# Deformable convolution on one core: the offsets' rows are requested from ScalarE instead of SP

## The chip, the cores and the metric

One core of one Trainium2 chip runs the whole kernel. The metric is the device time of one execution in microseconds (us); lower is better. Engines are named as in the profile: PE (TensorE), ACT (ScalarE), DVE (VectorE), POOL (GpSimd), SP (SyncE, which here only requests DMAs).

## The reference

The input `x` is 8 images of 32 channels by 128 x 128, float32. Two residual layers follow one another:

```
x = x + L0_conv(group_norm(x))     # a spectral layer: 16 modes along each axis, plus a 1x1 mix
x = x + L1_conv(group_norm(x))     # a modulated deformable 3x3 convolution
```

With 32 groups of one channel, the group norm is a norm over each channel plane. The second layer first makes, with a plain 3x3 convolution `w_om`, 27 numbers for each pixel: two offsets and one mask value for each of the 9 taps. It then samples the image bilinearly at the offset place of each tap, multiplies by sigmoid(mask), and sums over taps and channels with `weight`. This second layer takes nearly all of the time, and the change is in it.

## The kernel before, in words

The images are cut into 2 groups of 4 images, and 4 images x 32 channels fill 128 partitions. A first stage (up to about 280 us) loads both groups, makes the first layer's output `x1`, stores it to DRAM (`x1_d`), and stores the normalised rows with a zero border to DRAM as `xh_d` (tensor `xh_scratch` in the profile).

The second layer then walks over sets. A set is 2 image rows of a group (`TILE_R = 2`). There are `NSET = 65` sets for a group (64 pairs of rows and one that only finishes), so 130 in all. Each engine has its own function `step(N, ...)` which is called for N = -3 to 130. The helper `steps` writes the first and last few steps out ("peeled") and puts the rest into a loop. The engines are tied together by semaphores only; each engine does its own instructions in the order in which they are written. In PE's step N (L1085 to L1110) the work for several sets is woven together:

- `gather` (L1026, 64 matmuls, 4 times a step) applies the sampling weights to the transposed tiles, and `spread` (L1005, 64 matmuls, 3 times) makes those weights' layout; `turn_rows` (L1035, 4 times) transposes image tiles.
- `convolve(N - 1)` (L1080, 144 matmuls) is the last product of set N - 1.
- `offsets(N + 3)` (L1047, 24 recorded matmuls) comes right behind it: the 3x3 convolution for the offsets of the set three ahead, into the PSUM tile `pM`. It reads the SBUF buffer `wino`, which holds, for 3 row shifts, the rows of that set. `wino` is a part of the large tile `big`, so the profile calls its loads `big<-xh_scratch`. There is one such buffer.
- `turn_offsets(N + 3)` (L1057) brings the offsets into another order.

What the other engines do with it: ACT copies `pM` with a bias to `om_s` (L623), and in the same step copies results of `gather` (L588, `samples`), of `spread` (L593 and L594, `table`) and of `turn_rows` (L599, `turned`). DVE copies the other halves (L758, L763), transposes products (L769), and in `output(N - 1)` writes `outs` (L780) and `begun` (L785) from what `convolve(N - 1)` left. POOL cuts the image window into tiles (L502) and makes products (L490).

What sets the order around the change is SP's step. It requests everything that the second layer loads and stores, in one fixed order: the window of set N + 1 (L390), the rows of `x1` for set N (L418, two DMAs), the output rows of set N - 1 (L425, two DMAs, behind a wait for `outs`, L422), and last the rows for the offsets of set N + 3 (L402, three DMAs, behind a wait for `om_done`). That last part is

```python
wait(sp, om_done, n)
sp.nop(nofuse=True)
for ky in range(KS):
    rows = xh_d[g * P:(g + 1) * P, bass.ds(src + (TOP - 1 + ky) * PADC, TILE_R * PADC)]
    sp.dma_start(wino[ky * C:(ky + 1) * C, :, :, :] ...).then_inc(wino_ld, 16)
```

and PE waits for it with `pe.wait_ge(wino_ld, n * (16 * KS) + 16 * KS)` at L1043. `steps` has an argument `apart`: with True the loop is broken at the border between the two image groups and the steps around it are written out; SP and DVE used it, ACT, POOL and PE did not. At the border one step has no output to store.

Of the kernel before, what the change touches and what calls it, by code (L numbers as in the profile page):

```python
# [15 lines left out]
C = 32  # L16
H = W = 128
IPG = 4
P = IPG * C
HW = H * W  # L20
MODES = 16
KS = 3
# [4 lines left out]
TILE_R, TILE_C = 2, 4  # L27
# [3 lines left out]
TOP, LEFT = 3, 4  # L31
PADR = TOP + H + TOP
PADC = LEFT + W + LEFT
# [3 lines left out]
NSET = NPAIR + 1  # L37
# [24 lines left out]
RING = 4  # L62
# [10 lines left out]
def build(nc, g_count, x, wxr, wxi, wyr, wyi, mixt, mixb, womt, bom, wct, biasc,  # L73
          dft, inv, ident_d, perm, sel, cols, gtab, out):
    ctx = ExitStack()
    with ctx:
# [6 lines left out]
        def sem(name):  # L83
            return ctx.enter_context(nc.semaphore(name))
# [3 lines left out]
        xh_d = nc.dram_tensor("xh_scratch", (g_count * P, PADR * PADC), fp32, kind="Internal").ap()  # L88
# [18 lines left out]
        wino = areas[6].rearrange("p (b r x) -> p b r x", b=IPG, r=TILE_R)  # L107
# [112 lines left out]
        xh_st = [sem(f"xh_st{i}") for i in range(2)]  # L220
        pad_st = sem("pad_st")

        win_ld = [sem(f"win_ld{i}") for i in range(2)]
        wino_ld = sem("wino_ld")
        x1_ld = [sem(f"x1_ld{i}") for i in range(2)]
        out_st = [sem(f"out_st{i}") for i in range(2)]
        om_done = sem("om_done")
# [41 lines left out]
        N_XH = H // XHR  # L269
        SETS = g_count * NSET  # L270
# [3 lines left out]
        def wait(eng, s, v):  # L274

            if not (isinstance(v, int) and v <= 0):
                eng.wait_ge(s, v)
# [54 lines left out]
        def _(sp):  # L332
# [20 lines left out]
            for b in range(IPG):  # L353
                r, m = slice(b * C, (b + 1) * C), slice(b * C, b * C + OMC)
# [6 lines left out]
            for ky in range(KS):  # L361
                r, k = slice(ky * C, (ky + 1) * C), slice(ky * KS, (ky + 1) * KS)
# [28 lines left out]
                             xh_d[g * P:(g + 1) * P, bass.ds(local * (TILE_R * PADC), WIN_R * PADC)]) \  # L391
                    .then_inc(win_ld[q], 16)

            def load_rows(n, place):

                g, local = place(n)
                src = local * (TILE_R * PADC)
                wait(sp, om_done, n)
                sp.nop(nofuse=True)
                for ky in range(KS):  # L400
                    rows = xh_d[g * P:(g + 1) * P, bass.ds(src + (TOP - 1 + ky) * PADC, TILE_R * PADC)]
                    sp.dma_start(wino[ky * C:(ky + 1) * C, :, :, :].rearrange("c b r x -> c b (r x)"),  # L402
                                 rows.rearrange("(b c) n -> c b n", b=IPG)).then_inc(wino_ld, 16)

            def halves_of(t, g, pair, i):

                return t[g * P:(g + 1) * P, bass.ds(pair * PX + i * W, W)].rearrange("(r p) n -> p r n", r=2)

            def step(N, s, on, place):
                q = s % 2  # L410
                if on[1]:
                    load_window(N + 1, 1 - q, place)
                g, local = place(N)
                if on[0] and not (isinstance(local, int) and local == NPAIR):
                    wait(sp, conv_read, N - 1)
                    sp.nop(nofuse=True)
                    for i in range(TILE_R):
                        sp.dma_start(x1r[i * HALF:(i + 1) * HALF, q, :, :], halves_of(x1_d, g, local, i)) \  # L418
                            .then_inc(x1_ld[q], 16)
                g, local = place(N - 1)  # L420
                if on[-1] and not (isinstance(local, int) and local == 0):
                    sp.wait_ge(out_ready, N - 1 - g)  # L422
                    sp.nop(nofuse=True)
                    for i in range(TILE_R):
                        sp.dma_start(halves_of(out, g, local - 1, i), outs[i * HALF:(i + 1) * HALF, 1 - q, :, :]) \  # L425
                            .then_inc(out_st[1 - q], 16)
                if on[3]:
                    load_rows(N + 3, place)
            steps(sp, step, 2, True)
            for q in range(2):  # L430
                sp.wait_ge(out_st[q], 16 * NPAIR * g_count)
# [118 lines left out]
        @block.scalar  # L550
        def _(act):
            act.wait_ge(const_ld, 16 * NCONST)
            def deviation(g, n):
                act.wait_ge(aggr, n * g_count + g + 1)
                nc.scalar.activation(col1[:, g, 5 * n:5 * n + 1], mv[:, g, 1:2], ACT.Sqrt,
                                     bias=cols_s[:, 3:4]).then_inc(sd_done, 1)

            for g in range(g_count):
                deviation(g, 0)
            act.wait_ge(zeroed, 1)  # L560

            def normalize(g, j, q):

                nc.scalar.activation(
                    stg[:, q, :, LEFT:LEFT + W],
                    X[g][:, bass.ds(j * (2 * XHR * W) + q * XHR * W, XHR * W)]
                    .rearrange("p (a b) -> p a b", b=W),
                    ACT.Identity, bias=col1[:, g, 7:8], scale=col1[:, g, 6:7]).then_inc(xh_done, 1)

            for g in range(g_count):  # L570
                deviation(g, 1)
                act.wait_ge(norm1, g + 1)
                first = 0
                if g == 0:
                    for q in range(2):
                        normalize(g, 0, q)
                    first = 1
                with act.Fori(first, N_XH // 2) as j:
                    for q in range(2):
                        act.wait_ge(xh_st[q], (j + g * (N_XH // 2)) * 16)  # L580
                        normalize(g, j, q)
            act.wait_ge(x1_st, 16 * LOADS * g_count)
            act.wait_ge(blocks_ld, 16 * NBLOCK)

            def samples(n, k):

                act.wait_ge(v_done, n * TCH + (k + 1))
                nc.scalar.activation(*evacuate(k, 0), ACT.Copy).then_inc(v_act, 1)  # L588

            def table(n, j):  # L590

                act.wait_ge(e_done, n * ROUNDS + (j + 1))
                nc.scalar.activation(*unit_of(j, 0, 0), ACT.Copy)  # L593
                nc.scalar.activation(*unit_of(j, 1, 0), ACT.Copy).then_inc(e_act, 1)  # L594

            def turned(n, k):

                act.wait_ge(t_done, n * TCH + (k + 1))
                nc.scalar.activation(XT[:, k * 512:(k + 1) * 512], pR[:, :], ACT.Copy).then_inc(xt_done, 1)  # L599

            def step(N, s, on, place):
                if on[-1]:
                    samples(N - 1, 2)
                if on[0]:
                    table(N, 0)
                    turned(N, 2)
                if on[-1]:
                    samples(N - 1, 3)
                if on[2]:
                    act.wait_ge(sub_done, N + 3)  # L610
                    nc.scalar.activation(U, U, ACT.Abs).then_inc(abs_done, 1)
                if on[0]:
                    turned(N, 3)
                    table(N, 1)
                if on[2]:
                    act.wait_ge(abs_done, N + 3)
                    wait(act, prod_done, N * KS)
                    nc.scalar.activation(HT[:, :, (s + 2) % RING, :],
                                         U.rearrange("p (f n) -> p f n", f=2 * KS), ACT.Relu,
                                         bias=cols_s[:, 1:2], scale=-1.0).then_inc(lin_done, 1)  # L620
                if on[3]:
                    act.wait_ge(om_done, N + 4)
                    nc.scalar.activation(  # L623
                        om_s[:, :].rearrange("p (i j t) -> p i j t", i=TILE_R, t=NT),
                        pM[:, 0:PX].rearrange("p (i t j) -> p i j t", i=TILE_R, t=NT),
                        ACT.Identity, bias=bom_s[:, 0:1]).then_inc(om_act, 1)
                if on[0]:
                    samples(N, 0)
                    table(N, 2)
                if on[1]:  # L630
                    turned(N + 1, 0)
                if on[0]:
                    samples(N, 1)
                if on[1]:
                    turned(N + 1, 1)
                if on[3]:
                    act.wait_ge(omT_done, N + 4)
                    wait(act, hats_done, N + 2)
                    nc.scalar.activation(msk[:, 1 - s % 2, :], pM[:, 2 * KS * PB:3 * KS * PB],  # L639
                                         ACT.Sigmoid).then_inc(msk_done, 1)  # L640
            steps(act, step, RING)

            act.wait_ge(flag_set, 1)
            far = act.value_load(flag_i[0:1, 0:1], min_val=0, max_val=1)
            with act.If(far > 0):
                for i in range(images):
                    m = g_sem[i // IPG]
                    at0 = (i % IPG) * H
                    with act.Fori(0, H) as y:
                        act.wait_ge(m["own"], y * OWN + (at0 * OWN + 1))  # L650
                        nc.scalar.activation(g_mask, g_om[:, 2 * TAPS:OMC], ACT.Sigmoid).then_inc(m["act"], 1)
# [556 lines left out]
```

## Time and profile before

| | us |
|---|---|
| median of 2 runs (3114.12 to 3114.29) | 3114.2 |
| the profiled execution's own time | 3112.75 |
| its span, first to last instruction | 3110.7 |
| PE busy | 2128.6 (68%) |
| DVE busy | 1373.5 (44%) |
| ACT busy | 1159.8 (37%) |
| POOL busy | 890.1 (29%) |
| mean granted TensorE clock | 0.818 of full |

Busy time of an engine is the sum over its own instructions; the requests of DMAs are not counted in it. The mean granted clock is a share of 2.4 GHz. The second layer fills the span from about 280 us to the end.

### The profile page before, as it was taken

What the parts mean: (1) busy time and instruction counts of PE and PEld (TensorE: products, weight loads), DVE (VectorE), ACT (ScalarE), POOL (GpSimd) and SP (SyncE); (2) the same over time, 40 slices, a digit from 0 to 9 for tenths busy, and PEclk for the clock granted to TensorE, in tenths of its full rate; (3) what the DMA queues carried; (4) which work ended last, traced back from release to release, by engine and by line L of the source; (5) the groups of instructions that cost most, each with busy time, mean ns of one, the idle gap of its engine ahead of it and who ended that gap; (6) DMA issues with size and microseconds to landing.
All of it is one profiled execution on the core that took longest, in us unless ns stands there. A gap on an engine that the chain in (4) does not pass through costs nothing.

```text
span 3110.7 us, 187708 instructions
## 1 busy us (share of the span) xinstructions
PE 2128.6 (68%) x83517; PEld 1562.6 (50%) x83517; DVE 1373.5 (44%) x2326; ACT 1159.8 (37%) x2378; POOL 890.1 (29%) x1153
## 2 busy tenths in 40 slices
PE   7653666766767667676676767676676766767666
PEld 3312544555545555455555555455554555545454
DVE  9692333434434344344444444343443444434443
ACT  0024333433434344343443444343443434434343
POOL 0001223323233232332323332332323323233231
PEclk9795788888888887888878888888878888788888
DMA  6165112121121211212112111212112121121210
GB/s 238 58 249 187 37 45 57 42 56 50 49 56 42 56 49 49 56 42 56 49 50 55 55 50 49 56 42 56 49 49 56 42 56 49 50 56 42 56 50 25
DMA packets 161699, 196.30 MB, mean 63 GB/s; under 512 B 20288, under 2 KB 136672, under 8 KB 157536
## 3 DMA queue, kind: packets, MB, share of 16 engines
q1 hardware_dynamic: 161632, 195.34, 21.2%
q8 instruction: 50, 0.82, 0.1%
q14 instruction: 17, 0.14, 0.0%
HBM read 143.05 MB, written 52.22 MB: 63 GB/s over the span
## 4 chain that ended last, share of the span: by engine, by line
PE 55%; DMA 12%; issue 10%; SPq 10%; ACT 7%; DVE 6%; DVEq 1%; ACTq 0%
PE pE L1005 14%; PE pM L1047 12%; DMA big<-xh_scratch 11%; PE pVV L1026 10%; PE pVV L1080 9%; PE pR L1035 7%; SPq L425 6%; SPq L402 4%; ACT big L599 3%; ACT big L594 3%; PE pM L1057 2%; DVE outs L780 2%; DVE big L736 2%; DMA xh_scratch<-win 1%; DVEq L736 1%
## 5 line engine op out<-in xcount | busy, mean ns | idle before, releaser
L1047 PE MATMUL pM<-big,wom 96*32 96x256 f32 x3120 | 358.6, 628 | 826.0 <-DMA big<-xh_scratch 826.0
L502 POOL COPY big<-win 128x480 f32<-128x480 f32 x520 | 289.5, 587 | 1830.3 <-PE pR L1035 1817.6
L758 DVE COPY big<-pVV 128x288 f32<-128x288 f32 x520 | 232.7, 447 | 1223.2 <-PE pVV L1026 1222.9
L1047 PEld LDWEIGHTS pM<-big,wom 96*32 96x32 f32 x3120 | 128.7, 164 | 977.5 <-DMA big<-xh_scratch 791.6
L1026 PE MATMUL pVV<-big 60*32 60x72 f32 x33280 | 511.0, 253 | 16.7 <-issue 14.6
L623 ACT ACTIVATE om_s<-pM,bom_s 128x256 f32<-128x256 f32 x130 | 61.8, 476 | 1215.2 <-PE pM L1047 1215.2
L490 POOL TENSOR_TENSOR prod<-big 128x600 f32<-128x600 f32 (+1 forms) x489 | 504.1, 1040 | 0.0
L1026 PEld LDWEIGHTS pVV<-big 60*32 60x32 f32 x33280 | 407.9, 116 | 177.9 <-issue 172.2
L763 DVE COPY big<-pE 128x768 f32<-128x768 f32 x390 | 368.7, 945 | 229.7 <-PE pE L1005 229.7
L1005 PE MATMUL pE<-big,sel_s 32*64 32x96 f32 x24960 | 449.5, 274 | 20.4 <-issue 10.3
L1005 PEld LDWEIGHTS pE<-big,sel_s 32*64 32x64 f32 x24960 | 372.8, 145 | 86.7 <-issue 71.2
L769 DVE STREAM_TRANSPOSE big<-prod 128x768 f32<-128x768 f32 x390 | 377.6, 968 | 0.2 <-DVE outs L780 0.2
L1035 PE MATMUL pR<-ident,big 128*128 128x128 f32 x2080 | 362.8, 300 | 17.8 <-ACT big L599 1.6
L599 ACT ACTIVATE big<-pR 128x512 f32<-128x512 f32 x520 | 310.3, 597 | 43.2 <-PE pR L1035 38.3
L1080 PE MATMUL pVV<-big,wc 64*32 64x128 f32 x18720 | 297.5, 272 | 11.3 <-issue 10.5
L588 ACT ACTIVATE big<-pVV 128x288 f32<-128x288 f32 x520 | 214.0, 412 | 208.3 <-PE pVV L1026 204.5
L593 ACT ACTIVATE big<-pE 128x384 f32<-128x384 f32 x390 | 199.4, 511 | 232.9 <-PE pE L1005 232.9
L1035 PEld LDWEIGHTS pR<-ident,big 128*128 128x128 f32 x2080 | 232.1, 148 | 96.1 <-ACT big L599 54.5
L1080 PEld LDWEIGHTS pVV<-big,wc 64*32 64x32 f32 x18720 | 260.0, 106 | 29.5 <-issue 14.4
L594 ACT ACTIVATE big<-pE 128x384 f32<-128x384 f32 x390 | 195.4, 501 | 0.0
L780 DVE SCALAR_TENSOR_TENSOR outs<-pVV,bias_s,begun 128x256 f32<-128x256 f32 x128 | 61.9, 483 | 180.3 <-PE pVV L1080 180.3
L801 DVE TENSOR_TENSOR big<-pM,cols_s 128x720 f32<-128x720 f32 x130 | 116.7, 898 | 55.2 <-ACT msk L639 55.2
(75 smaller groups left out, 1147.7 us busy)
## 6 DMA issues: line engine op xcount, KB each, us to landing
big<-xh_scratch SPq DMA_DIRECT2D x390, 136.0 KB, 2.6
win<-xh_scratch SPq DMA_DIRECT2D x130, 408.0 KB, 3.5
xh_scratch<-win SPq DMA_DIRECT2D x32, 544.0 KB, 2.7
big<-in_x SPq DMA_DIRECT2D x16, 1024.0 KB, 15.7
x_scratch<-big SPq DMA_DIRECT2D x16, 1024.0 KB, 3.9
x1r<-x_scratch SPq DMA_DIRECT2D x256, 64.0 KB, 3.0
out<-outs SPq DMA_DIRECT2D x256, 64.0 KB, 2.1
xh_scratch<-zero SPq DMA_DIRECT2D x4, 204.0 KB, 2.7
```

What stands on the lines that cost most here:

```text
L490: made = nc.gpsimd.tensor_tensor(prod[:, kx, at:at + m, 0:SQ].rearrange("p m (a b) -> p m a b", a=NSH), hy.to_broadcast(shape), hx.to_broa ...
L502: last = nc.gpsimd.tensor_copy(strips[:, half * HTP:(half + 1) * HTP, h, 0:REG].rearrange("p t (r x) -> p t r x", r=WIN_R), tiles_of(q, h, ...
L594: nc.scalar.activation(*unit_of(j, 1, 0), ACT.Copy).then_inc(e_act, 1)
L599: nc.scalar.activation(XT[:, k * 512:(k + 1) * 512], pR[:, :], ACT.Copy).then_inc(xt_done, 1)
L758: nc.vector.tensor_copy(*evacuate(k, 1)).then_inc(v_dve, 1)
L763: nc.vector.tensor_copy(*both_units(j, 2)).then_inc(e_dve, 1)
L769: nc.vector.transpose(PT[:, kx, :], prod[:, kx, :, :].rearrange("p m k -> p (m k)")) \
L1005: last = mm(o[:, i2::TILE_R], sel_s[part, i2 * KS + kx, :], src[:, i2::TILE_R, :, t0:t0 + HTP], start=True, stop=True)
L1026: last = mm(o[:, :, t * TILE_C:(t + 1) * TILE_C, :], XT[part, x:x + C], A[part, at, :], start=True, stop=True)
L1035: last = nc.tensor.transpose(pR[:, u * P:(u + 1) * P], strips[:, k * TPC + u, :, :].rearrange("p h x -> p (h x)"), ident[:, :])
L1047: last = mm(pM[b * C:(b + 1) * C, 0:PX], wom[:, kx, :], wino[0:KS * C, b, :, x0:x0 + W], start=(kx == 0), stop=(kx == KS - 1))
L1080: last = mm(pV[r][to:to + C, c:c + W], wc[part, PLACES[at][1] * KS + kx, o * C:(o + 1) * C], VS[part, m, kx, :], start=(at == same[0] and ...
```

## The change

`load_rows` leaves SP's step and goes to ACT, right behind the copy of the offsets (L623). It is called for the next set, N + 4, so it is requested when `offsets(N + 3)` has finished reading the buffer, and no longer behind SP's output stores. The rows of set 0 are requested before ACT's first step. ACT's steps are now also written out at the border of the groups (`apart` is True), since the address depends on the group. PE, DVE and POOL are unchanged.

```diff
@@ SP
-            def load_rows(n, place):
-
-                g, local = place(n)
-                src = local * (TILE_R * PADC)
-                wait(sp, om_done, n)
-                sp.nop(nofuse=True)
-                for ky in range(KS):
-                    rows = xh_d[g * P:(g + 1) * P, bass.ds(src + (TOP - 1 + ky) * PADC, TILE_R * PADC)]
-                    sp.dma_start(wino[ky * C:(ky + 1) * C, :, :, :].rearrange("c b r x -> c b (r x)"),
-                                 rows.rearrange("(b c) n -> c b n", b=IPG)).then_inc(wino_ld, 16)
-
...
-                if on[3]:
-                    load_rows(N + 3, place)
             steps(sp, step, 2, True)
@@ ACT
+            def load_rows(n, place):
+
+                g, local = place(n)
+                src = local * (TILE_R * PADC)
+                for ky in range(KS):
+                    rows = xh_d[g * P:(g + 1) * P, bass.ds(src + (TOP - 1 + ky) * PADC, TILE_R * PADC)]
+                    nc.scalar.dma_start(wino[ky * C:(ky + 1) * C, :, :, :].rearrange("c b r x -> c b (r x)"),
+                                 rows.rearrange("(b c) n -> c b n", b=IPG)).then_inc(wino_ld, 16)
+
...
+            act.wait_ge(pad_st, 16 * 2 * g_count)
+            for q in range(2):
+                act.wait_ge(xh_st[q], 16 * (N_XH // 2) * g_count)
+            load_rows(0, lambda n: divmod(n, NSET))
 
             def step(N, s, on, place):
...
                         ACT.Identity, bias=bom_s[:, 0:1]).then_inc(om_act, 1)
+                    if not isinstance(N, int) or N + 4 < SETS:
+                        load_rows(N + 4, place)
                 if on[0]:
                     samples(N, 0)
...
-            steps(act, step, RING)
+            steps(act, step, RING, True)
```

## Rows read from the trace of the kernel before

**Rows 1.** The page: the chain that ended last, its shares by engine

```profile
PE 55%; DMA 12%; issue 10%; SPq 10%; ACT 7%; DVE 6%; DVEq 1%; ACTq 0%
```

**Rows 2.** The waits, 404.5 to 3034.05 us (us in total, times, longest)

```profile
PE pM L1047 <- DMA big<-xh_scratch: 765.2, 122, 6.6
```

**Rows 3.** The chain, 1634 to 1644 us (start us, us, what)

```profile
1634.91 2.21 PE pVV L1080 x144
...
1637.15 0.49 DVE outs L780
...
1637.71 0.63 SPq L425
...
1638.39 0.63 SPq L425
...
1639.11 0.55 SPq L402
...
1639.70 0.44 SPq L402
...
1640.19 2.81 DMA big<-xh_scratch
1643.00 0.04 issue
1643.04 2.79 PE pM L1047 x24
```

**Rows 4.** Windows: length; PE, PEld, DVE, ACT, POOL busy; granted clock, DMA share, GB/s

```profile
1617.00:1618.00 1.00, 0.00 (x0) 0.00 (x0) 0.08 (x1) 0.00 (x0) 0.00 (x0) 0.79 0.27 66
1741.37:1754.58 13.21, 12.99 (x643) 10.48 (x638) 8.84 (x13) 8.56 (x18) 7.04 (x11) 1.00 0.03 10
1621.33:1643.04 21.71, 15.61 (x638) 11.83 (x639) 9.04 (x14) 8.67 (x18) 6.68 (x8) 0.81 0.20 54
```

**Rows 5.** The timeline of the step at the border of the groups (start us, us)

```profile
1739.20 2.25 PE L1080 MATMUL pVV<-big,wc 64*32 64x128 f32 x144
...
1741.37 1.50 PE L1047 MATMUL pM<-big,wom 96*32 96x256 f32 x24
1741.50 0.43 DVE L785 TENSOR_TENSOR begun<-pVV,x1r 128x256 f32<-128x256 f32 x1 [1.24 <-PE pVV L1080]
1742.94 0.48 ACT L623 ACTIVATE om_s<-pM,bom_s 128x256 f32<-128x256 f32 x1 [1.97 <-PE pM L1047]
1743.81 0.41 ACT L588 ACTIVATE big<-pVV 128x288 f32<-128x288 f32 x1 [0.39 <-PE pVV L1026]
1744.70 0.51 ACT L593 ACTIVATE big<-pE 128x384 f32<-128x384 f32 x1 [0.48 <-PE pE L1005]
1745.11 0.51 ACT L594 ACTIVATE big<-pE 128x384 f32<-128x384 f32 x1
1745.48 0.61 ACT L599 ACTIVATE big<-pR 128x512 f32<-128x512 f32 x1
1746.14 0.66 PE L1035 MATMUL pR<-ident,big 128*128 128x128 f32 x4
1746.93 1.11 POOL L502 COPY big<-win 128x480 f32<-128x480 f32 x2 [3.75 <-PE pR L1035]
1752.36 2.25 PE L1080 MATMUL pVV<-big,wc 64*32 64x128 f32 x144
```

**Rows 6.** The timeline of SP, the same stretch and behind it

```profile
1729.59 1.28 SPq L402 DMA_DIRECT2D big<-xh_scratch  x3
1755.21 1.29 SPq L425 DMA_DIRECT2D out<-outs  x2
1756.60 1.52 SPq L402 DMA_DIRECT2D big<-xh_scratch  x3
1758.22 0.38 SPq L390 DMA_DIRECT2D win<-xh_scratch  x1
1758.69 1.31 SPq L418 DMA_DIRECT2D x1r<-x_scratch  x2
```

**Rows 7.** The page: DMA issues, KB each, median us from issue to landing

```profile
big<-xh_scratch SPq DMA_DIRECT2D x390, 136.0 KB, 2.6
win<-xh_scratch SPq DMA_DIRECT2D x130, 408.0 KB, 3.5
```

**Rows 8.** The timeline of PE: the ninth and the last of the 130 offsets' convolutions

```profile
432.49 2.79 PE L1047 MATMUL pM<-big,wom 96*32 96x256 f32 x24 [6.31 <-DMA big<-xh_scratch]
...
3034.05 2.79 PE L1047 MATMUL pM<-big,wom 96*32 96x256 f32 x24 [6.02 <-DMA big<-xh_scratch]
```

**Rows 9.** The timeline of PE, two waits for code in written-out steps

```profile
312.72 0.34 PE L1026 MATMUL pVV<-big 60*32 60x72 f32 x10 [1.64 <-issue]
...
3050.03 1.72 PE L1080 MATMUL pVV<-big,wc 64*32 64x128 f32 x100 [1.56 <-issue]
```

**Rows 10.** A window behind the first of them, columns as in rows 4

```profile
314.00:315.00 1.00, 1.00 (x36) 0.93 (x36) 0.00 (x0) 0.50 (x2) 1.00 (x3) 0.50 0.12 25
```

## Prediction

> **What bounds the kernel now.** I read the chain that ended last first. PE holds 55% of it, but DMA 12%, SP 10% and issue 10% also stand in it [rows 1], and a kernel bound by PE alone would have none of these. The waits say where they come from: in the loop PE sat idle 765.2 us in 122 waits for the rows of the offsets' convolution, so 6.27 us in each step [rows 2]. The chain of one step shows why [rows 3]. `convolve` ends at 1637.12. DVE writes `outs` (0.49 us), SP issues two output stores (1.3 us) and only then the three loads of rows, and the last one lands 2.81 us after its issue. At 1643.04 PE goes on, 5.9 us after it stopped. Nothing in the rows loaded depends on those outputs. SP's fixed order alone put them behind.
>
> The stall has a second cost. While PE is idle the granted clock falls (0.79 in a window inside the stall of another step), and the mean over a stalled step is 0.81 against 1.00 in a step without the stall [rows 4]. The convolution takes 2.79 us after a stall and 1.50 us without one [rows 3, 5].
>
> The border of the image groups is a natural experiment. There one step has no output to store, so SP requested the next rows early, at 1729.59 [rows 6], and at 1741.37 the convolution follows `convolve` at once [rows 5]. From that start to the start of the next `convolve` is 10.99 us, and from a `convolve` to the convolution behind it 2.17 us (1739.20 to 1741.37), so a step without the stall is 13.16 us. The mean step is (3034.05 - 432.49) / 121 = 21.50 us [rows 8]: from the ninth to the last of 130 convolutions.
>
> **The change, part by part.** All durations are of the profiled execution: span 3110.7 us, own time 3112.75, 1.45 below the median of 3114.2. So span + 2.05 + 1.45 compares with the median.
>
> *The stall goes.* The rows will be requested behind the offsets' copy, 1.57 us after `convolve` ends (1742.94 against 1741.37 [rows 5]), for use a full step later, some 11 us after the request. A load of rows lands 2.6 us after issue, the larger window load 3.5 [rows 7]. The stall of 6.27 us is gone, and so are the 2.07 us that a stalled step loses besides (21.50 - 13.16 - 6.27, the slow clock). The loop costs 121 x 13.16 = 1592.4 instead of 2601.6 us: 1009.2 saved, if nothing is added.
>
> *Outside the loop.* The steps ahead of it have four such waits, 6.31 us the last [rows 8], 24 us together. But their code is written out and PE also waits for code there, 1.56 and 1.64 us at a time [rows 9], and the stalls gave time to fetch it. I take 17 of the 24 (bounds 5 and 30), and 1.6 us for the warm clock behind the last convolution: 18.6.
>
> *SP.* The three issues (1.52 us) leave it [rows 6]. Window and `x1` loads move up by as much behind the outputs. What is late next there? POOL's tiles need the window 5.56 us after `convolve` ends (1746.93 - 1741.37 [rows 5]). SP will issue it at 0.6 + 1.3 + 0.1 = 2.0 us after that end, and it lands at 5.5, later if ACT's 408 KB share the way. A delay of 1 us costs nothing: POOL is busy 7 of 13.2 us [rows 4]. DVE's and POOL's work that now lies in the stall is `outs`, `begun`, a transpose and a product, and at the border the same transpose and product ran beside the convolution with no wait of PE. I cost this at 0.
>
> *ACT gets three issues.* No DMA is issued by ACT before, so I bound it. SP's three take 1.28 to 1.52 us, plus 0.1 to form addresses [rows 6]. Behind L623 ACT next owes L588, which it ran at 1743.81. L588 may start as late as 1744.3 (1744.70 less its 0.41) before it delays L593, and L593, L594, L599 are a tight chain on which the transpose at 1746.14 waits [rows 5]; each delay there is a delay of PE. If the issues start as L623 does, at 1742.94, they end at 1744.32 to 1744.56: up to 0.25 us lost. If they start when L623 has ended, at 1743.42, they end at 1744.8 to 1745.04: 0.5 to 0.75 lost. The bounds are 0 and 0.75 us a step, unless issuing is slower there than on SP. I take 0.4, the middle: x 121 = 48.4 us.
>
> L594 starts 0.40 us after L593, which lasts 0.51 [rows 5], so ACT's queue is ahead of its engine. The Trainium skill (Perfetto Trace Analysis, "DVE / Act Engine Instruction") says that the sequencer pushes an instruction into a wait queue and is then free for the next; by that rule the issues run beside L623 and the loss is the lower one, which would give about 2100 us; no run before shows it with a DMA.
>
> *The sum.* 3110.7 - 1009.2 - 18.6 + 48.4 = 2131.3 span, + 2.05 + 1.45 = 2135 us, 31% less. With a loss of 0 it is 2086, with 0.75 it is 2177: the forecast's own range is 2080 to 2180. The extra steps written out at the border for ACT (nine, little code) I cost at nothing; DVE and SP had them, and no wait of PE shows it.
>
> **The rivals.** *A. Issues of SP and ACT get in each other's way.* Before, one engine issued all; now SP issues stores, window and `x1` loads from 0.6 to about 3.7 us after `convolve` (1.29 + 0.38 + 1.31 with gaps [rows 6]), and ACT begins at 1.7. If one has to wait while the other issues, ACT's three wait for what is left of a store (0.25), the window (0.38) and one `x1` load (0.65): 1.3 us more. They end at 4.4 us, and L588's limit is 2.93 (1744.3 - 1741.37). The loss is 1.35 to 1.5 a step instead of 0.4. Time: 2086 + 121 x 1.35 = 2250 us. For it: in rows 6 no two issues ever lie over one another, but one engine made them all, so the trace can't tell. Against it: nothing. 
>
> *B. The clock stays low.* A single wait for code of 1.64 us [rows 9] was followed by a window at 0.50 [rows 10], although PE was busy in most of the time around it. If the smaller gaps left in each step do the same, the 2.07 us a step stay: 2135 + 250 = 2385 us. Against it: the border's step ran at 1.00 with ACT's short waits in it [rows 4].
>
> *C. Slower: ACT is held until its loads have landed.* Three times 2.6 us [rows 7] from 1.67 us on end at 9.5, 6.5 us past the limit of 2.93. PE would be idle as long as now, at another place, and the clock fall with it: 13.16 + 6.5 + 2.07 = 21.7 us a step, against 21.50: about 3140 us. With the window's 3.5 us each it is 24.4 us a step and 3465. It decides from 6.3 us of delay on ACT. For it: only that no issue on ACT was ever seen. Against: on SP an issue (0.5 us) returns long before the landing.
>
> *D. The rows are late all the same.* Landing would have to take 11 us instead of 2.6. Nothing speaks for it; then it stays near 3114.
>
> **How the numbers follow.** Forecast 0.62, A 0.23, B 0.08, C 0.03, D 0.02; 0.02 is left for a time under 2080. The predicted time is the forecast's 2135. The range takes in the forecast and A: 2075 to 2255. Faster by over 2% (which is about what a measurement of this kernel can tell from no change) are all but C and D: 0.95. D and the mild half of C are within 2%: 0.03. Slower: 0.02.
>
> **What would show it.** In the profile after, the wait of PE L1047 for the DMA is gone in the loop, L1047 takes 1.50 us, the mean clock is above 0.97, and a step is 13.2 to 13.9 us. PE L1035 waits for ACT L599 some tenths of a us once a step; that is the loss I took as 0.4, and its size tells the two bounds apart. Under A ACT's three issues last over 2.5 us instead of 1.5, in alternation with SP's, and the step is 14.5 us. Under B the step is over 15 us with a clock near 0.85. I am wrong altogether if PE's wait for DMA comes back under another name, such as POOL's for the window leading to PE's, or if PE's time in a step without waits isn't 13.2 us.

## The result and the profile after

| | before | after |
|---|---|---|
| median, us | 3114.2 (2 runs) | 2102.1 (2101.17 to 2103.03, 2 runs) |
| span of the profiled execution | 3110.7 | 2099.3 |
| mean granted TensorE clock | 0.818 | 0.96 |

The ratio is 0.6748, with a 95% interval of 0.6732 to 0.6764: the changed kernel takes a third less time. 2135 us was predicted, in a range of 2075 to 2255. One execution below is left aside: the first profile of e3_act_late was taken in a slow state (2996.9 us at a granted clock of 0.672), where the five other executions of that kernel took 2937 to 2950 us.

First the page of the kernel after: busy times, and the chain that ended last by engine.

```profile
PE 1876.1 (89%) x83517; PEld 1449.4 (69%) x83517; DVE 1372.3 (65%) x2326; ACT 1144.4 (55%) x2378; POOL 888.6 (42%) x1153
...
PE 58%; ACT 14%; issue 11%; ACTq 6%; DVE 5%; DMA 2%; DVEq 2%; SPq 0%; POOL 0%; POOLq 0%
```

Where [rows 1] had DMA with 12% and SP with 10%, there are now 2% and 0%. PE's busy time itself fell, from 2128.6 to 1876.1 us, for the same 83517 matmuls: that is the clock. ACT has 14% instead of 7%.

The waits of the kernel after, over its loop (413.16 to 2024.96 us, from the ninth to the last convolution), those that matter:

```profile
POOL big L489 <- DMA win<-xh_scratch: 715.6, 120, 7.8
...
PEld pR L1038 <- ACT big L595: 58.5, 230, 0.3
```

PE's wait for the rows [rows 2] isn't in this list at all. PE still waits for ACT's copy L595 (L599 of the kernel before), about half a microsecond a step in its weight loads, but that is no price of the change: the loop of a kernel in which ACT issues nothing (e11, below) has 57.4 us of it. POOL now waits for the window, which it did not before; that costs the kernel nothing, as below.

Windows of the kernel after, columns as in rows 4: a step in the loop, a step near the border that is written out, and the whole loop.

```profile
1106.76:1120.18 13.42, 12.99 (x643) 10.49 (x639) 8.97 (x14) 8.45 (x18) 6.65 (x9) 1.00 0.31 82
1239.28:1252.44 13.16, 12.98 (x642) 10.52 (x638) 8.98 (x14) 8.52 (x18) 6.84 (x10) 1.00 0.30 83
413.16:2024.96 1611.80, 1574.16 (x77203) 1271.20 (x77199) 1085.69 (x1692) 1022.94 (x2178) 819.54 (x1058) 1.00 0.30 82
```

The mean step is 1611.80 / 121 = 13.32 us against 21.50, at full clock. The written-out step takes exactly the 13.16 that the border's step of [rows 5] gave. Only ACT's, SP's and DVE's code is written out there; PE's and POOL's is still the loop.

The timeline of that written-out step, to set beside [rows 3, 5]:

```profile
1239.28 1.50 PE L1050 MATMUL pM<-big,wom 96*32 96x256 f32 x24
...
1239.96 1.30 SPq L414 DMA_DIRECT2D out<-outs  x2
...
1240.85 0.47 ACT L624 ACTIVATE om_s<-pM,bom_s 128x256 f32<-128x256 f32 x1 [1.97 <-PE pM L1050]
1240.85 1.35 ACTq L578 DMA_DIRECT2D big<-xh_scratch  x3
...
1241.35 0.55 SPq L390 DMA_DIRECT2D win<-xh_scratch  x1
...
1242.25 0.41 ACT L584 ACTIVATE big<-pVV 128x288 f32<-128x288 f32 x1 [0.93 <-PE pVV L1029]
...
1242.61 0.51 ACT L589 ACTIVATE big<-pE 128x384 f32<-128x384 f32 x1
...
1243.09 0.93 PE L1029 MATMUL pVV<-big 60*32 60x72 f32 x64
...
1246.98 1.12 POOL L489 COPY big<-win 128x480 f32<-128x480 f32 x2 [5.76 <-DMA win<-xh_scratch]
```

Three things are to be seen. The convolution (1.50 us) stands right behind `convolve`. ACT's three issues begin at the same instant as the copy L624 and end at 1242.20, after its engine has long been free; L584 starts at 1242.25, 0.05 us behind them, and early enough for PE's second `gather` (L1029), which stands 3.81 us behind the start of the convolution, as in the border's step before (1745.18 against 1741.37):

```profile
1745.18 0.89 PE L1026 MATMUL pVV<-big 60*32 60x72 f32 x64
```

And ACT's first issue lies over SP's store, which ended at 1241.26: both engines are issuing at the same time.

The same place in a step of the loop:

```profile
1108.33 0.48 ACT L624 ACTIVATE om_s<-pM,bom_s 128x256 f32<-128x256 f32 x1 [1.97 <-PE pM L1050]
1108.58 1.37 ACTq L578 DMA_DIRECT2D big<-xh_scratch  x3
...
1110.05 0.41 ACT L584 ACTIVATE big<-pVV 128x288 f32<-128x288 f32 x1 [1.25 <-PE pVV L1029]
...
1110.82 0.87 PE L1029 MATMUL pVV<-big 60*32 60x72 f32 x64 [0.18 <-issue]
```

Here the issues start 0.25 us behind the copy's start instead of with it; in most steps of the loop it is 0.15 to 0.16. In the loop the address is formed from the loop's register, and the trace has register instructions of L578 there; in a written-out step the address is a constant, and it has none. L584 starts 1.72 us behind L624 instead of 1.40, and the second `gather` 4.06 us behind the convolution's start (1106.76) instead of 3.81.

This is the whole loss. In 115 of the 121 steps from the ninth copy of the offsets to the last, a step takes the time from L624 to L584 plus 11.70 us, to within 0.03: 13.27 us with 1.57, 13.35 with 1.65, 13.41 with 1.71. Where L584 comes within 1.46 us, the step is 13.15 to 13.17.

### The profile page after: what moved, and what is told of

It is laid out like the page before. It is cut to its first block, busy times and chain, and to the rows that moved or that the text cites. A ratio compares the mean times of both kernels' runs of the same rounds, so it can differ in the third digit from the quotient of the medians.

```text
span 2099.3 us, 187393 instructions
## 1 busy us (share of the span) xinstructions
PE 1876.1 (89%) x83517; PEld 1449.4 (69%) x83517; DVE 1372.3 (65%) x2326; ACT 1144.4 (55%) x2378; POOL 888.6 (42%) x1153
## 4 chain that ended last, share of the span: by engine, by line
PE 58%; ACT 14%; issue 11%; ACTq 6%; DVE 5%; DMA 2%; DVEq 2%; SPq 0%; POOL 0%; POOLq 0%
PE pE L1008 14%; PE pVV L1083 14%; PE pM L1050 9%; PE pR L1038 9%; PE pVV L1029 8%; ACTq L578 6%; ACT big L595 5%; ACT big L590 5%; PE pM L1060 4%; DVE big L739 3%; ACT big L589 3%; DMA xh_scratch<-win 1%; DVEq L739 1%; DVE stats L674 1%; DMA win<-xh_scratch 1%
## 5 line engine op out<-in xcount | busy, mean ns | idle before, releaser
L1029 PE MATMUL pVV<-big 60*32 60x72 f32 x33280 | 469.2, 231 | 33.5 <-issue 26.5
L1029 PEld LDWEIGHTS pVV<-big 60*32 60x32 f32 x33280 | 377.0, 106 | 144.9 <-issue 138.3
L1008 PE MATMUL pE<-big,sel_s 32*64 32x96 f32 x24960 | 413.3, 255 | 17.0 <-issue 7.6
L1008 PEld LDWEIGHTS pE<-big,sel_s 32*64 32x64 f32 x24960 | 341.1, 131 | 73.5 <-issue 46.7
L1038 PE MATMUL pR<-ident,big 128*128 128x128 f32 x2080 | 345.4, 289 | 20.2 <-ACT big L595 1.9
L584 ACT ACTIVATE big<-pVV 128x288 f32<-128x288 f32 x520 | 214.0, 412 | 267.0 <-PE pVV L1029 255.4
L595 ACT ACTIVATE big<-pR 128x512 f32<-128x512 f32 x520 | 311.7, 599 | 38.9 <-PE pR L1038 38.3
L1038 PEld LDWEIGHTS pR<-ident,big 128*128 128x128 f32 x2080 | 220.9, 142 | 97.0 <-ACT big L595 62.0
L1050 PE MATMUL pM<-big,wom 96*32 96x256 f32 x3120 | 199.3, 387 | 52.1 <-DMA big<-xh_scratch 50.2
L624 ACT ACTIVATE om_s<-pM,bom_s 128x256 f32<-128x256 f32 x130 | 61.8, 475 | 272.8 <-PE pM L1050 272.8
L1050 PEld LDWEIGHTS pM<-big,wom 96*32 96x32 f32 x3120 | 88.3, 109 | 125.4 <-issue 76.5
L804 DVE TENSOR_TENSOR big<-pM,cols_s 128x720 f32<-128x720 f32 x130 | 116.7, 898 | 57.4 <-ACT msk L642 57.4
```

Source lines behind the costliest of these rows:

```text
L1008: last = mm(o[:, i2::TILE_R], sel_s[part, i2 * KS + kx, :], src[:, i2::TILE_R, :, t0:t0 + HTP], start=True, stop=True)
L1029: last = mm(o[:, :, t * TILE_C:(t + 1) * TILE_C, :], XT[part, x:x + C], A[part, at, :], start=True, stop=True)
L1038: last = nc.tensor.transpose(pR[:, u * P:(u + 1) * P], strips[:, k * TPC + u, :, :].rearrange("p h x -> p (h x)"), ident[:, :])
L1050: last = mm(pM[b * C:(b + 1) * C, 0:PX], wom[:, kx, :], wino[0:KS * C, b, :, x0:x0 + W], start=(kx == 0), stop=(kx == KS - 1))
```

## The experiments

The theory after the result: the gain is that the rows are asked for before the outputs are waited for, whoever asks; PE's own 13.16 us are then the floor of a step, and the 0.16 above it is ACT's address work and issues, which use up all of ACT's slack behind the offsets' copy. The rival: the second queue, ACT's, is what helps.

**e1_sp_head** and **e2_sp_before_out**: only SP's order, on the kernel before.

```diff
             def step(N, s, on, place):
                 q = s % 2
+                if on[3]:                      # e1_sp_head
+                    load_rows(N + 3, place)
                 if on[1]:
                     load_window(N + 1, 1 - q, place)
...
                         sp.dma_start(x1r[...]) .then_inc(x1_ld[q], 16)
+                if on[3]:                      # e2_sp_before_out
+                    load_rows(N + 3, place)
                 g, local = place(N - 1)
...
-                if on[3]:
-                    load_rows(N + 3, place)
             steps(sp, step, 2, True)
```

> The kernel before, but SP requests the offsets' rows at the head of its step, one set's time earlier, instead of last; ACT issues nothing and isn't written out at the border. Theory (the gain is that the rows are requested before the outputs are waited for, whoever issues): PE's wait for the rows goes, the step is 13.16 us and not the 13.32 of the changed kernel, since ACT has no issues on it: 121 x 0.16 = 19 us under the 2102 of the changed kernel, about 2085. Rival (a second queue is needed, because SP's three issues more delay the window or the x1 rows until PE waits for them): over 2150.

> As e1_sp_head, but the rows are requested behind the window and the x1 rows, just ahead of the wait for the outputs: the smallest edit of SP's order. Theory: the same 2085, and POOL's wait for the window is shorter than in e1_sp_head, because the window is requested first. Rival (the window's landing matters): this one is faster than e1_sp_head by over 10 us.

Measured: e1 2085.3 us (ratio 0.6705, 0.6694 to 0.6716), e2 2081.2 us (0.6687, 0.6675 to 0.6698). Both are where the theory put them, and the rival is out: SP alone, with no other queue, has the whole gain. The mean step is 13.21 and 13.18 us. e2 is 4 us faster, not 10, and the two intervals overlap, though in e1 POOL waits 9.8 us at worst for its window and in e2 4.9.

**e3_act_late**, run again as **e9_act_late_again**: the change's other half alone. ACT issues, but late, for set N + 3 and behind the outputs.

```diff
-            load_rows(0, lambda n: divmod(n, NSET))
...
                 if on[3]:
+                    wait(act, om_done, N + 3)
+                    g, local = place(N - 1)
+                    if on[-1] and not (isinstance(local, int) and local == 0):
+                        act.wait_ge(out_ready, N - 1 - g)
+                    act.nop(nofuse=True)
+                    load_rows(N + 3, place)
                     act.wait_ge(om_done, N + 4)
...
-                    if not isinstance(N, int) or N + 4 < SETS:
-                        load_rows(N + 4, place)
```

> The changed kernel, but ACT requests the rows late again: those of set N + 3, behind a wait for the outputs of set N - 1. So only the issuer is changed. Theory (the issuer is worth only the 1.3 us of SP's two stores, which no longer stand ahead): PE's stall is 0.6 + 1.35 + 2.6 = 4.6 us, with the slow clock's 2.07 behind it a step is 19.8 us: about 2900. Rival (ACT's own queue is what helps): near 2100.

> The kernel of e3_act_late once more, whose two times lay 60 us apart at a granted clock of 0.672 in the profile. Theory: undisturbed, the stall is 4.6 us and the slow clock's 2.07 us comes with it as in the kernel before, 2900 to 2940, mean clock near 0.80. Rival (a stall at this place costs more than before): it stays at 2970 or above.

Measured: 2937.2 us the first time and 2942.3 (2938.4 to 2949.8) the second, ratio 0.9459 (0.9443 to 0.9475), 2 us above the range that was expected. The timeline of the second:

```profile
1237.14 2.25 PE L1086 MATMUL pVV<-big,wc 64*32 64x128 f32 x144
1239.54 0.48 DVE L786 SCALAR_TENSOR_TENSOR outs<-pVV,bias_s,begun 128x256 f32<-128x256 f32 x1 [1.33 <-PE pVV L1086]
1240.24 1.41 ACTq L578 DMA_DIRECT2D big<-xh_scratch  x3
1240.25 1.49 SPq L414 DMA_DIRECT2D out<-outs  x2
...
1242.66 1.49 SPq L407 DMA_DIRECT2D x1r<-x_scratch  x2
1243.88 2.79 PE L1053 MATMUL pM<-big,wom 96*32 96x256 f32 x24 [4.49 <-DMA big<-xh_scratch]
```

The stall is 4.49 us (4.6 expected) with the convolution at 2.79 us again. The mean step of the loop is 20.00 us (19.8 expected). So to change the issuer alone is worth 5%, 1.5 us a step, about the length of SP's stores; to ask early is worth the rest. This timeline also settles rival A: the three issues of ACT and the two of SP run fully beside one another. ACT's take 1.41 us, where SP's three took 1.28 and 1.52 alone [rows 6]. SP's two take 1.49, more than the 1.29 of rows 6, but not because of ACT: the next pair, L407, takes 1.49 as well, 1 us after ACT's last issue ended, and the median of one store issue is 0.65 us in this kernel and in the kernel before.

**e4_apart_only**: the kernel before with only ACT's steps written out at the border (`steps(act, step, RING, True)`).

> The kernel before with only ACT's steps written out at the border of the groups. Theory: no change, 3110 to 3118. Rival (fetching ACT's extra code costs or helps): off by more than 10 us.

Measured: 3111.75 us, ratio 1.0004 (0.9993 to 1.0014), as expected. It costs nothing.

**e5_six_halves**: each of ACT's loads in two, by images.

```diff
                 for ky in range(KS):
-                    rows = xh_d[g * P:(g + 1) * P, ...]
-                    nc.scalar.dma_start(wino[ky * C:(ky + 1) * C, :, :, :] ...)
+                    for h in range(2):
+                        rows = xh_d[g * P + h * 64:g * P + (h + 1) * 64, ...]
+                        nc.scalar.dma_start(wino[ky * C:(ky + 1) * C, 2 * h:2 * h + 2, :, :] ...)
...
-                pe.wait_ge(wino_ld, n * (16 * KS) + 16 * KS)
+                pe.wait_ge(wino_ld, n * (32 * KS) + 32 * KS)
```

> The changed kernel with each of ACT's three loads cut into two (six issues, the same bytes). Theory (ACT's slack behind L624 is used up by three issues, so that every further 0.1 us there is 0.1 us of PE): if an issue has a fixed cost of 0.45 us, six take 2.7, 1.35 more, and the time is 2102 + 121 x 1.35 = 2265; if half of it goes with the rows moved, 2180. Rival (ACT has slack to spare): 2102 to 2115.

Measured: 2356.8 us, 255 more than the changed kernel and 92 over the highest number expected. Its timeline:

```profile
1245.57 0.47 ACT L625 ACTIVATE om_s<-pM,bom_s 128x256 f32<-128x256 f32 x1 [1.97 <-PE pM L1051]
1245.72 3.03 ACTq L579 DMA_DIRECT2D big<-xh_scratch  x6
...
1248.79 0.41 ACT L585 ACTIVATE big<-pVV 128x288 f32<-128x288 f32 x1 [2.75 <-issue]
...
1249.56 0.88 PE L1030 MATMUL pVV<-big 60*32 60x72 f32 x64 [1.68 <-ACT big L585]
```

Six issues of half the rows take 3.03 us in this step, and 2.83 us in many others of the loop; three of whole rows take 1.36 to 1.37 in most steps of the changed kernel's loop. That is 0.47 to 0.50 us an issue against 0.46, so the price is for the issue and hardly for the rows. PE waits 1.68 us for ACT's copy, in the second `gather`. The rule of the changed kernel holds here too: 14.72 us a step with L585 3.02 us behind the copy. On the mean L585 starts 3.18 us behind it instead of 1.62, which makes 188 of the 257 us that the loop is longer: the theory's 1.35 a step, a little larger. The rest, 68 us, is the clock. Two windows of the same kernel, one with the end of that gap (1249.56) in it and one 2.4 us behind that end:

```profile
1249.00:1250.00 1.00, 0.44 (x43) 0.47 (x46) 0.18 (x1) 1.00 (x4) 0.00 (x0) 1.00 0.99 327
1252.00:1253.00 1.00, 1.00 (x43) 0.93 (x48) 0.00 (x0) 0.23 (x1) 1.00 (x3) 0.50 0.00 0
```

In 54 of the 121 steps the clock falls to half behind the gap and in 67 it does not. The first take 16.22 us on the mean, the others 14.82, and together 15.44. The expectation had left that out.

**e6_copy_beside** and **e7_copy_behind**: one more copy on ACT, which nobody reads, before or behind the three issues.

```diff
+                    nc.scalar.activation(spare[:, :, :], wc[:, 0:4, :] ..., ACT.Copy)    # e6
                     if not isinstance(N, int) or N + 4 < SETS:
                         load_rows(N + 4, place)
+                    nc.scalar.activation(spare[:, :, :], wc[:, 0:4, :] ..., ACT.Copy)    # e7
```

> The changed kernel with one more ACT copy of 128x256 (some 0.45 us), which nobody reads, between the offsets' copy and the three issues. Theory (issues run beside ACT's engine, and L584 waits for the issues, not for the engine): the copy is done before the issues are, so it costs nothing, 2100 to 2112. Rival (issues start only when ACT's engine is done): + 121 x 0.45 = 2156.

> The same copy behind the three issues, ahead of L584. Theory (no slack is left there): each 0.4 us goes to PE: 2102 + 121 x 0.4 = 2150. Rival (slack to spare): 2102 to 2115.

Measured: e6 2107.3 us (ratio 0.6772, 0.6760 to 0.6783), e7 2140.6 us (0.6876, 0.6865 to 0.6888), 9 less than the 2150 expected. Of e6 and e7 in turn:

```profile
1245.36 0.48 ACT L625 ACTIVATE om_s<-pM,bom_s 128x256 f32<-128x256 f32 x1 [1.97 <-PE pM L1052]
1245.37 0.35 ACTq L579 DMA_DIRECT2D big<-xh_scratch  x1
1245.73 0.41 ACT L629 ACTIVATE spare<-wc 128x256 f32<-128x256 f32 x1
1245.76 0.97 ACTq L579 DMA_DIRECT2D big<-xh_scratch  x2
```

```profile
1248.97 0.47 ACT L625 ACTIVATE om_s<-pM,bom_s 128x256 f32<-128x256 f32 x1 [1.97 <-PE pM L1052]
1248.97 1.53 ACTq L579 DMA_DIRECT2D big<-xh_scratch  x3
1250.56 0.42 ACT L631 ACTIVATE spare<-wc 128x256 f32<-128x256 f32 x1 [1.11 <-issue]
```

In e6 the engine runs the extra copy while the queue issues, and the kernel pays nothing that can be told (13.35 us a step, and the changed kernel, run again, 13.34). In e7 the copy waits for the issues, and the step is 13.63 us: 0.3 more for a copy of 0.42. So behind the offsets' copy it is ACT's queue, not its engine, that has no slack left.

**e8_pe_wait**: PE waits for `begun` before the convolution (`wait(pe, conv_read, n - 3)` in `offsets`).

> The changed kernel, but PE waits for DVE's begun (L788) of the same step before the offsets' convolution, so it idles some 0.95 us in each step. Theory (a wait this short costs its own length, the clock stays up): 2102 + 128 x 0.95 = 2220, mean clock over 0.95. Rival B of the prediction (short waits keep the clock low): the clock falls to about 0.82 and the time is 2220 + 250 = 2470.

Measured: 2245.2 us, mean clock 0.96. A step:

```profile
1255.69 1.50 PE L1051 MATMUL pM<-big,wom 96*32 96x256 f32 x24 [1.11 <-DVE begun L788]
```

That is 25 us more than expected: the idle time is 1.11 us in this step and 1.20 in nearly half of them, not 0.95, the mean step 14.49 (1.17 over 13.32), and 121 x 1.17 = 142 of the 143 us are explained by it. The clock stays up, at 1.00 in the loop. Rival B is out for waits of this length.

**e10_after_again** and **e11_sp_again**: the changed kernel and e2's, side by side in five rounds.

> The changed kernel again, to stand beside the next one on the same chip: 2100 to 2106.

> The kernel of e2_sp_before_out again, the version that may beat both: 2079 to 2085, so 0.8 to 1.1% under the changed kernel, in every step of the loop 13.16 us against 13.32 (theory: ACT forming the addresses of its issues in the loop is what the 0.16 us are). Rival (the difference between chips or jobs made it): no difference.

Measured: 2106.05 us (ratio 0.6768, 0.6758 to 0.6777) and 2082.18 us (0.6690, 0.6681 to 0.6699). The intervals are apart; the reordered SP is 1.1% faster than the change. The mean steps are 13.342 and 13.178 us, and 121 x 0.164 = 19.8 of the 23.9 us lie in the loop. Another 3.7 us lie ahead of the first convolution, which starts at 284.44 us in e10 and at 280.74 in e11.

```profile
1240.94 0.47 ACT L623 ACTIVATE om_s<-pM,bom_s 128x256 f32<-128x256 f32 x1 [1.97 <-PE pM L1047]
...
1241.83 0.41 ACT L588 ACTIVATE big<-pVV 128x288 f32<-128x288 f32 x1 [0.41 <-PE pVV L1026]
...
1243.48 1.49 SPq L402 DMA_DIRECT2D big<-xh_scratch  x3
```

This is e11: L588 waits for PE again and not for issues, and the rows are requested as SP's last work before it waits for the next outputs, 2.5 us after the offsets' copy began and 9 us ahead of the convolution that reads them (1252.53), where a load lands 2.6 us after its issue (median). In 120 of the 121 steps of e11 the time is 13.15 to 13.18 us, in the loop as well as at the border: with no issues on ACT the 0.16 are gone.

## Why the prediction was right, point by point

*The stall and the clock behind it go: right.* The step taken from the border, 13.16 us, was met to the hundredth in seven of the nine written-out steps, and in nearly every step of e2 and e11. 6.27 us of waiting and 2.07 of slow clock were both real, and e9 shows them come back together when the stall does. The convolution takes 1.50 us, and the clock over the loop is 1.00.

*ACT's three issues: right that they delay what stands behind them, too large in size, and wrong in the way to PE.* This is the one term that was mis-sized. "I take 0.4, the middle" stood for 48.4 us; measured are 1611.8 - 1592.4 = 19.4, or 0.16 us a step. The issues run beside the copy (e6), so the lower bound, 0 to 0.25, was the right one of the two, and I was wrong to sit between it and its opposite.

The sentence on the wait queue, from the Trainium skill (Perfetto Trace Analysis, "DVE / Act Engine Instruction"), would have given 2100 us. The trace agrees with it on what counted here, that the issues run beside the copy. It does not agree that ACT's sequencer was free from the moment it had pushed the copy: ACT had sat idle for 1.97 us in the steps shown, the copy waiting for PE, and in all 121 steps the first thing behind it, an issue or the forming of its address, began 0.01 us after the copy began and never before. The loads have no wait of their own for the end of `offsets`; in these steps the copy's wait holds them back.

The way to PE was another one than I gave. I took the chain L593, L594, L599 and the transpose at 1746.14 to be late next, and named PE's wait for L599 as the sign by which to read off the loss. That wait is there without any issue on ACT (57.4 us in e11's loop, 58.5 in the changed kernel's), so it tells nothing. What comes late is PE's second `gather`, at 1745.18 in the border's step, which I did not look at and which cannot start before L588 (now L584) has copied the first one's result; in e5 the trace names it ([1.68 <-ACT big L585]). That L588's limit was nearly right, 1.36 us behind the copy (1744.3) where the steps give 1.46, was luck.

What the 0.16 consist of the timelines say, and no kernel took it out alone. In the loop the first issue comes 0.15 us, in some steps 0.25, behind the start of the copy, since its address is formed first, and in a third of the steps the three then take 1.45 us instead of 1.36. In the written-out steps they start at once. Two of the nine written-out steps lose time all the same (13.32 and 13.31 us): in them the second issue takes 0.69 and 0.71 us instead of 0.47, and the trace does not show why.

*Outside the loop: near.* Before, 3110.7 - 2601.6 = 509.1 us lay outside the loop, after, 2099.3 - 1611.8 = 487.5. The gain is 21.6 us where 18.6 were taken. It is a sum of gains and a loss that I had not thought of: the first convolution starts at 284.29 us instead of 280.99. ACT's first loads now go out at 277.09 together with SP's two windows and `x1` rows, where before SP sent them first; that they share the way is the likely reason, and was not tested alone. How much of the gain is the time for fetching code, as I argued, stays open: the trace names no cause for the waits of [rows 9].

*The sum.* Of the 33 us between 2135 and 2102, 29 are ACT's term, 3 what lies outside the loop, and 1 the distance from span to median (2.8 us instead of 3.5).

*SP and the window: right in cost, wrong in time.* I had the window land 5.5 us after `convolve`, "later if ACT's 408 KB share the way". It lands 4.8 us after its issue (median) instead of 3.5, and POOL starts on it at 1246.98, 7.6 us after `convolve` ended (1239.35). POOL loses 2 us and not the 1 that I let pass, and it is still free: in e11 the window lands after 3.3 us, and the written-out steps of both kernels are 13.16.

*Rival A fell.* Issues of SP and ACT overlap (e9), and ACT's three last 1.35 us, not over 2.5. The Trainium skill (Perfetto Trace Analysis, "DMA Instruction — HWDGE") has the generator of descriptors locked by one issue at a time; where it differs from the timeline, the timeline decides: no lock long enough to make one engine wait out the other's issue is seen. A small one can't be excluded: the median issue of rows takes 0.34 us on ACT and took 0.32 on SP. SP's window issue behind the store took 0.55 us instead of 0.38 in the step shown, but that is not ACT's doing: in e11, where ACT issues nothing, the same issue takes 0.55 at the same place (1241.45).

*Rival B fell* for the changed kernel (clock 1.00 in the loop) and at 1.11 us of idle a step (e8), but e5 shows that it starts not far above. *C and D fell*: ACT's queue was free again 1.35 us after it began, where a load took 2.6 us to land before [rows 7], and no wait for rows is left.

## What to carry to other kernels

Look at what stands ahead of a load in its issuing engine's fixed order. A load that depends on nothing recent but is queued behind a wait for the newest result starts with that result, and its latency is then exposed in every step; moving it ahead of that wait, on the same engine, is worth the stall and also the slow clock that follows the stall. If an engine with computing to do is to issue it instead, count its slack behind the instruction before, at about 0.45 us an issue and 0.15 to 0.25 for the first address in a loop, and look for the first of the other engines' instructions that waits for what comes behind: here it was PE's second `gather`, and SP's reordering alone was 1.1% better than the move to ACT. And look for a step in which the obstacle happens to be missing (the border's step): it gives the time after the change before anything is changed.

## What the runs showed of the hardware that was not expected

A DMA issue on ACT costs about as much as on SP (three in 1.35 us against 1.28 to 1.52) and hardly depends on its size: 0.46 us for 128 rows of 1088 bytes, 0.47 to 0.50 for 64 (e5). Issues of the two engines run at the same time (e9). An issue that stands behind an ACT copy runs beside the copy but does not start before it, in any of 121 steps. And the clock's answer to gaps in PE's work is not even: 1.1 to 1.2 us idle in each step left it at 1.00 (e8). In e5, where the longest gap of a step was 1.3 to 2.1 us, it fell in 54 of 121 steps: in 4 of the 45 with a gap of 1.4 to 1.6 us, in 32 of the 42 with 1.7 to 1.8, and not in the one of 2.1. With 4.5 us (e9) the convolution behind the gap took 2.7 to 2.8 us in every step but the border's.
